# The key mask moved into the score accumulation, and two instead of three expert-sum buffers with smaller prefetch windows

## The chip, the cores and the metric

The kernel runs on one core of one Trainium2 chip. The metric is the device time of one execution in microseconds (us). Engines are named as the profile does: PE is TensorE's matmul, PEld its weight load, DVE is VectorE, ACT is ScalarE, POOL is GpSimd and SP is SyncE, whose instructions are almost all DMA issues ("q" behind an engine's name is its sequencer).

## The reference, cut to what matters

Four layers of gated cross attention and feed-forward run over `x` of shape (16, 128, 256), 2048 tokens, in float32. The two places that the change touches are the first attention (layer 0, 16 heads over 128 keys per sample, with a key mask that is all true in the inputs) and the last feed-forward (layer 3, 64 experts, top 8, capacity-limited):

```python
x = x + jnp.tanh(g_xattn[0]) * _L0_xattn_ref(_layernorm(x, axis=-1), ctx_1024, mask_BxS2_bf1, Wq, Wk, Wv, Wo)
...
# layer 3 feed-forward
xe = jnp.zeros((E, C, H), x.dtype).at[flat_e, pos].set(x_rep, mode='drop')
gu = jnp.einsum('ech,ehf->ecf', xe, gate_up_proj)
g, u = jnp.split(gu, 2, axis=-1)
h = jax.nn.silu(g) * u
ye = jnp.einsum('eci,eih->ech', h, down_proj)
y = jnp.sum(y_flat.reshape(-1, K, H) * topw.reshape(-1, K)[..., None], axis=1)
```

In the layer-0 attention a masked key's score is driven to a huge negative number before the softmax; `any_key` zeroes a sample without a single valid key.

## The kernel before, in words

The work is one long program; each engine has its own instruction stream, written out in order by hand, and the streams meet at counting semaphores (`done(engine, signal, body, item)` waits for one item of a signal). Nothing is planned at run time.

**Layer-0 attention** (`wide_pe`, `wide_act`, `wide_dve`, `wide_pool`, run by `wide_run` for `L0`). Tokens are taken in four blocks `s` of 512 (four samples), and each block has 16 heads, so there are 64 steps of one head on one block. Step `t` is a software pipeline: PE makes the q of head `t` (two float32 matmuls of 512 columns, into bank B4), transposes the probabilities of head `t-4` (line 552), makes the scores of head `t-1` (four matmuls of 128 columns into the four quarters of bank B5, line 565), adds head `t-5` to the output Y (two matmuls of 512 columns), and makes o of head `t-4` (four matmuls of 128). All matmuls are recorded at the helper's line 129, transposes at their own. DVE then adds the mask to the whole bank B5 in place (line 686), takes the maximum over keys (line 687) and scales it (line 693); ACT takes the exponentials (line 635); DVE makes the reciprocal sums; POOL normalizes (line 722). Each DVE result is followed by a wait on its own chain semaphore (`link`). PE may overwrite B5 only once `p_ready` of the head before has come, that is, after ACT has read B5. The mask, as a bf16 additive bias on all 128 partitions, is made once at the start (line 3187) from a copy of the mask bytes broadcast to 128 partitions.

**Zeroing of internal DRAM tables** (`rows_init`): at the start SP queues plain DMAs that blank the row tables and the sum buffers of the three routed feed-forwards. SP then waits for the end of the layer-0 attention before it goes on.

**Layer-3 feed-forward** (`f3_sp`, `f3_pe`, `f3_act`, `f3_dve`, `f3_pool`). Experts 0 to 63 are taken in order. For expert `e`, SP loads its 128 routed rows (row width 324 floats) into slot `e % XR` of `f3_xe` (XR = 12; line 2744); before it does, it waits until the sum of expert `e - XR` has landed. PE transposes the rows (line 2902), makes gate and up, later the down product; ACT copies and takes silu (lines 2926, 2932); DVE multiplies (line 2939) and scales the result into slot `e % YR` of `f3_y` (YR = 4; line 2946), for which it waits until the sum of expert `e - 4` has landed. POOL then issues an indirect DMA that adds the 128 result rows into an internal DRAM buffer `acc[e % AC]` (AC = 3; line 2892). Two additions into one buffer may not be under way together, so POOL waits before expert `e` until the addition of expert `e - AC` has landed. This "scatter-add" is what the text calls a scatter. Expert weights sit in 16 slots (GE = 16), the first 16 experts' are loaded long before, and the rest are loaded by SP in groups of QE = 2 experts between the row loads (lines 2727 and 2729), each group once the last expert that used its slots is through. At the end SP reads the three buffers back in four parts (12 loads, line 2754), DVE adds them (line 2954, two additions a part), adds the gated sum to x (line 2956), and SP stores the output (line 2758).

Of the kernel before, what the change touches and what calls it, by code (L numbers as in the profile page):

```python
# [14 lines left out]
P = 128  # L15
# [36 lines left out]
def _build(nc, ctx, a, out):  # L52
# [56 lines left out]
    ident = sb("ident", [P, P])  # L109
    gates = sb("gates", [P, 8])  # L110
# [44 lines left out]
    mask_bias = tile(R2, 17000, 1024).bitcast(BF16)  # L155

# [125 lines left out]
    class Wide:  # L282


        def __init__(self, name, stage, kv_heads, wq, wk, wv, wo, rms):
# [22 lines left out]
            self.chain = signal("attn_chain", HEADS * (2 if rms else 4))  # L308
# [225 lines left out]
    def wide_pe(pe, S, beside=None):  # L534
# [4 lines left out]
        for t in S.steps:  # L539
# [112 lines left out]
    def wide_dve(dve, S, beside=None):  # L652
        A, s = S.A, S.s

        link = S.chain(dve, A.chain, 1 if A.rms else 6, s)
        if S.ahead or S.old_ahead:
            k_link = Chain(dve, A.k_chain, s + 1, -1 if S.old_ahead else 0)
        for t in S.steps:
# [23 lines left out]
            if S.has(h):  # L682
                i = h % 2
                done(dve, A.s_mm, s, h)
                if not A.rms:
                    link(nc.vector.tensor_tensor(B5, B5, mask_bias[:, tok(S.of(h))], ALU.add))
                link(nc.vector.tensor_reduce(mx[:, i, :], B5.rearrange("p (b k) -> p b k", b=TB), AX.X, ALU.max))  # L687
                if A.rms:
                    done(dve, A.rq_ready, s, h)
                    nc.vector.scalar_tensor_tensor(negm[:, i, :], mx[:, i, :], -1.0, rq[:, i, :], ALU.mult, ALU.mult)\  # L690
                        .then_inc(A.negm_ready.sem, 1)
                else:
                    nc.vector.tensor_scalar(negm[:, i, :], mx[:, i, :], -SCALE_WIDE, None, ALU.mult)\  # L693
                        .then_inc(A.negm_ready.sem, 1)
# [767 lines left out]
    AC = 3  # L1462
    xrows = nc.dram_tensor("f3_rows", (SLOTS, ROW3), F32, kind="Internal").ap()
    acc = [nc.dram_tensor(f"moe_sum{i}", ((B + 1) * P, D), F32, kind="Internal").ap() for i in range(AC)]
    xrows_of = xrows.rearrange("(p e) c -> p e c", e=L3E)
    tables_of_rows = [(F.dram.rearrange("(b p) c -> p b c", p=P), F.acc) for F in (F1, F2)] + [(xrows_of, acc)]
    row_inits = 16 * sum(len(sums) + -(-rows.shape[1] // ROW_BLOCKS) for rows, sums in tables_of_rows)
# [7 lines left out]
    def rows_init(sp, rows, sums):  # L1475
# [3 lines left out]
        for sum_of in sums:  # L1479
            sp.dma_start(sum_of.rearrange("(b p) d -> p b d", p=P), row_blank[:, 0:D].unsqueeze(1).broadcast_to([P, B + 1, D]))\  # L1480
                .then_inc(rows_zeroed, 16)
# [1167 lines left out]
    XR = 12  # L2649
# [3 lines left out]
    QE = 2  # L2653
# [8 lines left out]
    class R3:  # L2662
# [34 lines left out]
    f3_sum = [tile(R1, i * B * D, B * D).rearrange("p (b d) -> p b d", b=B) for i in range(AC)]  # L2697
# [13 lines left out]
    rows_sems = [(x.sem, x.end) for x in kb_in + F2.tile_in[2:]] + [(semaphore(f"f3_rows_in{i}"), 0) for i in range(XR - TG)]  # L2711
    f3_rows_in = [Signal(sem, 16 * -(-L3E // XR), 1, base) for sem, base in rows_sems]
    f3_added = [Signal(sem, 16 * -(-(L3E - i) // AC), 1, base) for i, (sem, base) in
                enumerate([(x.sem, x.end) for x in F2.added] + [(semaphore("f3_added2"), 0)])]
# [23 lines left out]
    def f3_sp(sp):  # L2738
        for sig in rows_written:
            sp.wait_ge(sig.sem, sig.end)  # L2740
        for e in range(L3E):
            if e >= XR:
                done(sp, f3_added[(e - XR) % AC], 0, 16 * ((e - XR) // AC) + 15)
# [5 lines left out]
        for sig in f3_added:  # L2749
            sp.wait_ge(sig.sem, sig.end)  # L2750
# [136 lines left out]
    def f3_pool(pool):  # L2887
        for e in range(L3E):
            done(pool, f3_y_ready, 0, e)
            if e >= AC:  # L2890
                done(pool, f3_added[e % AC], 0, 16 * (e // AC) - 1)
            nc.gpsimd.indirect_dma_start(acc[e % AC], bass.IndirectOffsetOnAxis(ap=f3_xe[:, e % XR, D:D + 1].bitcast(U32), axis=0),
                                         f3_y[:, e % YR, :], None,
                                         bounds_check=(B + 1) * P - 1, compute_op=ALU.add).then_inc(f3_added[e % AC].sem, 16)
# [39 lines left out]
    def f3_dve(dve):  # L2934
        for j in range(L3E + 2):
# [13 lines left out]
    def f3_end_dve(dve):  # L2949
        for j in range(NS):  # L2950
            b = slice(j * TB, (j + 1) * TB)
            dve.wait_ge(sum_in[j], 64 + 16 * AC)
            for i in range(1, AC):
                nc.vector.tensor_tensor(f3_sum[0][:, b], f3_sum[0][:, b], f3_sum[i][:, b], ALU.add).then_inc(sum_chain, 1)
                dve.wait_ge(sum_chain, j * (AC - 1) + i)
# [6 lines left out]
    def _(sp):  # L2962
# [3 lines left out]
        mask = a["mask_BxS2_bf1"].rearrange("b k -> (b k)").rearrange("(o n) -> o n", o=1)  # L2966
        sp.dma_start(mask_all, mask.broadcast_to([P, B * P])).then_inc(in_small, 16)
# [113 lines left out]
    def _(pe):  # L3081
# [9 lines left out]
        pe.wait_ge(const_made, 1)  # L3091
# [41 lines left out]
    def _(act):  # L3133
        act.wait_ge(go, 1)
        act.wait_ge(in_small, 48)
# [41 lines left out]
    def _(dve):  # L3177
# [8 lines left out]
        dve.wait_ge(in_small, 48)  # L3186
        nc.vector.tensor_scalar(mask_bias, mask_all, 1.0, NEG_BIG, ALU.subtract, ALU.mult).then_inc(mask_ready, 1)
# [54 lines left out]
```

## Time and profile before

| what | value |
|---|---|
| median of 3 runs | 2602.42 us (2602.17 to 2604.09) |
| the profiled execution's own time | 2602.42 us |
| its span, first to last instruction | 2600.7 us |
| PE busy | 2179.0 us (84%) |
| DVE busy | 1282.5 us (49%) |
| ACT busy | 1143.6 us (44%) |
| POOL busy | 1058.1 us (41%) |
| mean granted TensorE clock | 0.931 of full speed |

The row loads' line in the page gives KB each and the median us from issue to landing. The span leaves out 1.7 us that lie around the first and last instruction. Busy time on PE is modelled from pipelined records, so neighbouring records overlap: the distance between two starts says what a matmul costs, its duration does not. The layer-0 attention lies between about 66 and 430 us of the span, the layer-3 feed-forward between about 2412 and 2601 us.

### The profile page before, as it was taken

The numbers are of one execution on the slowest core, as the hardware profiler recorded it, in microseconds if no ns is written. First come the engines' busy times: TensorE is split into PE (matmuls) and PEld (weight loads), VectorE is DVE, ScalarE is ACT, GpSimd is POOL, SyncE is SP. The second block draws the span as 40 slices with busy tenths as digits, with TensorE's granted clock in tenths as the row PEclk, the third lists the DMA queues.
The fourth block names the chain that finished last, engine by engine and source line by source line (L and its number), as shares of the span: only waits on it lengthen the run. The fifth ranks groups of instructions, "written<-read, shape, count | busy, mean of one in ns | idle before, by whom it ended". The sixth has DMA issues, their size and how long they took to land.

```text
span 2600.7 us, 37681 instructions
## 1 busy us (share of the span) xinstructions
PE 2179.0 (84%) x11449; PEld 1517.5 (58%) x11449; DVE 1282.5 (49%) x3474; ACT 1143.6 (44%) x3509; POOL 1058.1 (41%) x899
## 2 busy tenths in 40 slices
PE   5999999789999978959999999888995788771773
PEld 4566666657667645636666566446663566551663
DVE  2545554466766663336565554343335365552223
ACT  3444444245545543335665555223332575550221
POOL 1112211033344344534444544324555337656564
PEclk9999999899999998979999999899997899885887
DMA  9999200200000033630000000335667002110898
GB/s 351 358 350 335 81 1 1 66 1 1 1 18 16 3 89 72 100 107 1 1 1 10 27 14 23 120 116 97 102 105 178 9 9 73 62 46 2 200 239 203
DMA packets 218720, 233.18 MB, mean 90 GB/s; under 512 B 31451, under 2 KB 210419, under 8 KB 217756
## 3 DMA queue, kind: packets, MB, share of 16 engines
q1 hardware_dynamic: 181276, 182.62, 23.3%
q0 software_dynamic: 37248, 48.14, 10.1%
q8 instruction: 98, 1.61, 0.3%
q14 instruction: 98, 0.80, 0.1%
HBM read 95.36 MB, written 143.85 MB: 92 GB/s over the span
## 4 chain that ended last, share of the span: by engine, by line
PE 25%; issue 9%; POOL 8%; DVE 6%; DMA 5%; ACT 2%; SPq 1%; POOLq 0%; DVEq 0%; ACTq 0%
PE ps L129 20%; POOL f_rows L2784 4%; DMA moe_sum<-work 4%; POOL weights L2629 2%; PE ps L552 1%; PE ps L578 1%; PE ps L1870 1%; PE ps L1885 1%; POOL rk L437 1%; DMA f_rows<-ctx,weights 1%; ACT work L635 1%; PE ps L406 1%; PE ps L1635 0%; SPq L2754 0%; DVE mx L687 0%
## 5 line engine op out<-in xcount | busy, mean ns | idle before, releaser
L129 PE MATMUL ps<-weights,work 128*128 128x126 f32 (+7 forms) x3328 | 701.4, 344 | 55.5 <-DVE work L2946 29.6
L129 PEld LDWEIGHTS ps<-weights,work 128*128 128x128 f32 (+2 forms) x3328 | 472.4, 195 | 114.5 <-issue 59.9
L129 PE MATMUL ps<-work,weights 128*128 128x512 f32 (+3 forms) x1456 | 494.1, 466 | 3.2 <-ACT work L644 3.2
L129 PE MATMUL ps<-xn_T,weights 128*128 128x512 f32 (+5 forms) x1056 | 381.6, 496 | 12.8 <-DVE weights L1146 6.7
L129 PEld LDWEIGHTS ps<-work,weights 128*128 128x128 f32 (+2 forms) x1456 | 224.6, 189 | 88.1 <-issue 74.8
L1948 POOL DMA_INDIRECT f_sum<-work x120 | 184.9, 1541 | 191.7 <-ACT work L1909 148.9
L722 POOL TENSOR_TENSOR work<-work,rinv 128x512 f32<-128x512 f32 x128 | 133.3, 1042 | 296.6 <-DVE rinv L670 273.6
L129 PEld LDWEIGHTS ps<-xn_T,weights 128*128 128x128 f32 (+3 forms) x1056 | 166.7, 189 | 113.7 <-issue 96.4
L1018 POOL TENSOR_TENSOR work<-weights,head_sel 128x512 f32<-128x512 f32 x128 | 134.3, 1053 | 228.2 <-PE ps L129 200.3
L968 ACT ACTIVATE work<-ps,n_negm 128x128 f32<-128x128 f32 x512 | 145.6, 371 | 133.6 <-DVE n_negm L995 130.2
L635 ACT ACTIVATE work<-ps,negm,rq 128x128 f32<-128x128 f32 x256 | 113.8, 454 | 148.6 <-DVE negm L690 148.6
L129 PE MATMUL ps<-weights 128*128 128x256 f32 (+6 forms) x546 | 148.2, 395 | 22.6 <-DMA weights<-weights 7.3
L635 ACT ACTIVATE work<-ps,negm 128x128 f32<-128x128 f32 x256 | 90.6, 366 | 151.8 <-DVE negm L693 151.8
L2784 POOL DMA_INDIRECT f_rows<-ctx,weights x128 | 128.7, 1006 | 57.2 <-issue 38.2
L129 PEld LDWEIGHTS ps<-work 128*128 128x128 f32 x1024 | 129.6, 192 | 34.5 <-issue 31.6
L993 DVE TENSOR_REDUCE n_mx<-ps 128x4 f32<-128x512 f32 x128 | 88.2, 689 | 116.6 <-PE ps L129 115.0
L2487 ACT ACTIVATE work<-ps,n_negm 128x112 f32<-128x112 f32 (+1 forms) x512 | 112.9, 346 | 72.4 <-DVE n_negm L2556 72.3
L728 POOL TENSOR_TENSOR rq<-qvar,neg_half 128x4 f32<-128x4 f32 x64 | 68.7, 1074 | 185.8 <-DVE qvar L699 185.7
L678 DVE COPY work<-ps 128x512 f32<-128x512 f32 x128 | 88.3, 690 | 100.4 <-PE ps L552 99.8
L129 PE MATMUL ps<-work 128*128 128x128 f32 x1024 | 135.4, 275 | 1.8 <-DVE work L678 1.8
L1560 POOL DMA_INDIRECT f_rows<-xn,weights x96 | 98.6, 1027 | 75.5 <-DVEq L1549 51.4
L2629 POOL TENSOR_TENSOR weights<-weights,neg_half 128x32 f32<-128x32 f32 x16 | 87.1, 5443 | 98.0 <-DVE weights L2581 98.0
(313 smaller groups left out, 3538.5 us busy)
## 6 DMA issues: line engine op xcount, KB each, us to landing
f_rows<-weights SPq DMA_DIRECT2D x25, 2176.0 KB, 19.6
work<-f_rows SPq DMA_DIRECT2D x120, 136.0 KB, 2.5
weights<-in_L_ffn_gate_up_proj SPq DMA_DIRECT2D x32, 384.0 KB, 4.9
f_rows<-weights SPq DMA_DIRECT2D x4, 2592.0 KB, 24.8
work<-f_rows SPq DMA_DIRECT2D x64, 162.0 KB, 4.4
f_sum<-weights SPq DMA_DIRECT2D x4, 2176.0 KB, 16.4
weights<-in_L_ffn_W SPq DMA_DIRECT2D x96, 88.0 KB
moe_sum<-weights SPq DMA_DIRECT2D x3, 2176.0 KB, 17.9
```

Of the source, the lines that this page charges most:

```text
L129: return nc.tensor.matmul(out, lhsT, rhs, start=start, stop=stop, skip_group_check=True)
L635: last = nc.scalar.activation(p_sb[:, h % 4, b * P:(b + 1) * P], B5[:, b * P:(b + 1) * P], ACT.Exp, bias=negm[:, h % 2, b:b + 1], scale=rq ...
L678: nc.vector.tensor_copy(pt_sb, B6).then_inc(A.pt_ready.sem, 1)
L722: nc.gpsimd.tensor_tensor(out=pv, in0=pv, in1=rinv[:, h % 2, :].unsqueeze(2).broadcast_to([P, TB, P]), op=ALU.mult).then_inc(A.pn_ready.se ...
L968: last = nc.scalar.activation(n_p[:, i, j, :], S_BANKS[t % 3][:, j * P:(j + 1) * P], ACT.Exp, bias=n_negm[:, i, j:j + 1], scale=scale)
L993: link(nc.vector.tensor_reduce(n_mx[:, t % 4, 0:NB], S_BANKS[t % 3].rearrange("p (h k) -> p h k", h=NB), AX.X, ALU.max))
L1018: nc.gpsimd.tensor_tensor(out=s_kblk[:, g % KB_RING, :, :], in0=k_t[:, hf, b * P:(b + 1) * P].unsqueeze(1).broadcast_to([P, NB, P]), in1=h ...
L1560: nc.gpsimd.indirect_dma_start(F.dram, bass.IndirectOffsetOnAxis(ap=F.slot_u[:, t, k:k + 1], axis=0), XN[:, t, :], None, bounds_check=F.ro ...
L1948: nc.gpsimd.indirect_dma_start(F.acc[j % 2], bass.IndirectOffsetOnAxis(ap=t_xe[:, j, D:D + 1].bitcast(U32), axis=0), t_y[:, j % 4, :], Non ...
L2487: last = nc.scalar.activation(n_p[:, i, j, lo:hi], S_BANKS[t % 3][:, j * P + lo:j * P + hi], ACT.Exp, bias=n_negm[:, i, m:m + 1], scale=SC ...
L2629: nc.gpsimd.tensor_tensor(out=l3_r[:, b % 2, :], in0=l3_var[:, b % 2, :], in1=neg_half[:, 0:32], op=ALU.pow)\
L2784: nc.gpsimd.indirect_dma_start(xrows, bass.IndirectOffsetOnAxis(ap=f3_slot_u[:, s % 2, t, k:k + 1], axis=0), f3_rows[s % 2][:, t, :], None ...
```

## The change

There are two independent edits.

In the layer-0 attention the addition of the mask on DVE is gone. PE instead opens the accumulation in bank B5 with one bf16 matmul of 512 columns, whose stationary operand is a 128 by 128 tile that holds ones in partition 0 and zeros elsewhere (`ones_b`), and whose moving operand is the mask bias of the block, now filled in partition 0 only and zero elsewhere. The four score matmuls add to it. The start of the program has one DMA more (the mask as a single row), and DVE three small fills more.

In the layer-3 feed-forward there are two sum buffers instead of three, 8 row slots instead of 12, and weights come in groups of 4 experts instead of 2. The row slots and sums have their semaphores accordingly; the end reads and adds two buffers.

```diff
@@ wide_pe
                 done(pe, A.p_ready, s, i - 1)
                 if A.rms:
                     done(pe, A.k_ready, s, i // 4 * 4 + 3)
+                else:
+                    mm(B5, ones_b[:], mask_bias[:, tok(S.of(i))], True, False)
...
-                    last = mm(B5[:, b * P:(b + 1) * P], q_sb[:, i % 2, b * P:(b + 1) * P], keys)
+                    last = mm(B5[:, b * P:(b + 1) * P], q_sb[:, i % 2, b * P:(b + 1) * P], keys, A.rms, True)
@@ wide_dve
                 done(dve, A.s_mm, s, h)
-                if not A.rms:
-                    link(nc.vector.tensor_tensor(B5, B5, mask_bias[:, tok(S.of(h))], ALU.add))
                 link(nc.vector.tensor_reduce(mx[:, i, :], B5.rearrange("p (b k) -> p b k", b=TB), AX.X, ALU.max))
@@ rows_init
-    acc = [... for i in range(AC)]
+    acc = [... for i in range(2)]
@@ layer 3, sizes
-    XR = 12
+    XR = 8
...
-    QE = 2
+    QE = 4
@@ f3_sp
             if e >= XR:
-                done(sp, f3_added[(e - XR) % AC], 0, 16 * ((e - XR) // AC) + 15)
+                done(sp, f3_added[e % 2], 0, 16 * ((e - XR) // 2) + 15)
             sp.dma_start(f3_xe[:, e % XR, :], xrows_of[:, e, :]).then_inc(f3_rows_in[e % XR].sem, 16)
...
-            for i in range(AC):
+            for i in range(2):
                 sp.dma_start(f3_sum[i][:, b], ...).then_inc(sum_in[j], 16)
@@ f3_pool
             done(pool, f3_y_ready, 0, e)
-            if e >= AC:
-                done(pool, f3_added[e % AC], 0, 16 * (e // AC) - 1)
-            nc.gpsimd.indirect_dma_start(acc[e % AC], ...
+            done(pool, f3_added[e % 2], 0, 16 * (e // 2) - 1)
+            nc.gpsimd.indirect_dma_start(acc[e % 2], ...
@@ f3_dve
                 if e >= YR:
-                    done(dve, f3_added[(e - YR) % AC], 0, 16 * ((e - YR) // AC) + 15)
+                    done(dve, f3_added[e % 2], 0, 16 * ((e - YR) // 2) + 15)
@@ f3_end_dve
-            for i in range(1, AC):
-                nc.vector.tensor_tensor(f3_sum[0][:, b], f3_sum[0][:, b], f3_sum[i][:, b], ALU.add).then_inc(sum_chain, 1)
+            nc.vector.tensor_tensor(f3_sum[0][:, b], f3_sum[0][:, b], f3_sum[1][:, b], ALU.add).then_inc(sum_chain, 1)
@@ start, SP
+        sp.dma_start(mask_row[0:1, :], mask).then_inc(in_small, 16)
         sp.dma_start(mask_all, mask.broadcast_to([P, B * P])).then_inc(in_small, 16)
@@ start, DVE
-        dve.wait_ge(in_small, 48)
-        nc.vector.tensor_scalar(mask_bias, mask_all, 1.0, NEG_BIG, ALU.subtract, ALU.mult).then_inc(mask_ready, 1)
+        nc.vector.memset(mask_bias, 0.0)
+        nc.vector.memset(ones_b[:], 0.0).then_inc(const_made, 1)
+        dve.wait_ge(const_made, 2)
+        nc.vector.memset(ones_b[0:1, :], 1.0).then_inc(const_made, 1)
+        dve.wait_ge(in_small, 64)
+        nc.vector.tensor_scalar(mask_bias[0:1, :], mask_row[0:1, :], 1.0, NEG_BIG, ALU.subtract, ALU.mult).then_inc(mask_ready, 1)
```

## Rows read from the trace of the kernel before

**Rows 1.** The page: DMA busy in tenths over 40 slices, and the row loads' issues.

```profile
DMA  9999200200000033630000000335667002110898
...
work<-f_rows SPq DMA_DIRECT2D x64, 162.0 KB, 4.4
```

**Rows 2.** Windows: stretch, busy of PE, PEld, DVE, ACT, POOL, granted clock, DMA share, GB/s.

```profile
160.00:250.00 90.00, 90.00 (x454) 59.42 (x453) 47.66 (x126) 42.98 (x157) 18.22 (x18) 1.00 1.09 345
2440.00:2540.00 100.00, 75.92 (x486) 68.06 (x485) 28.85 (x82) 25.00 (x82) 62.57 (x41) 0.88 1.01 242
```

**Rows 3.** Timeline of one layer-0 step, PE and DVE: start, us, engine, line.

```profile
199.78 1.88 PE L129 MATMUL ps<-xn_T,weights 128*128 128x512 f32 x4
...
201.50 0.60 PE L552 MATMUL ps<-ident,work 128*128 128x128 f32 x4
...
201.94 1.06 PE L129 MATMUL ps<-ctx_T,work 128*128 128x128 f32 x8
...
202.83 1.88 PE L129 MATMUL ps<-work,weights 128*128 128x512 f32 x4
203.03 0.70 DVE L686 TENSOR_TENSOR ps<-ps,weights 128x512 f32<-128x512 f32 x1 [0.20 <-PE ps L129]
...
204.55 1.05 PE L129 MATMUL ps<-work 128*128 128x128 f32 x8
...
205.44 1.88 PE L129 MATMUL ps<-xn_T,weights 128*128 128x512 f32 x4
```

**Rows 4.** Timeline, PE at the scores of heads 1 and 3 of block 0.

```profile
72.62 1.13 PE L129 MATMUL ps<-ctx_T,work 128*128 128x128 f32 x8 [1.64 <-ACT work L635]
...
81.58 1.13 PE L129 MATMUL ps<-ctx_T,work 128*128 128x128 f32 x8 [1.19 <-ACT work L635]
```

**Rows 5.** PE groups by shape, 160 to 250 us, and the widest bf16 group: busy, mean ns.

```profile
L129 PE MATMUL ps<-work,weights 128*128 128x512 f32 x63 | 29.7, 593 | 0.0
...
L129 PE MATMUL ps<-weights 128*128 128x64 bf16 x40 | 2.7, 204 | 4.3 <-DVE weights L2862 2.3 <-DVE x_res L2602 2.0
```

**Rows 6.** Timeline of the start: DVE at the mask, PE at the first weights.

```profile
14.59 1.23 DVE L3187 TENSOR_SCALAR weights<-work 128x2048 bf16<-128x2048 uint8 x1 [3.98 <-DMA gates<-in_g_ffn]
...
27.93 1.97 PE L334 MATMUL ps<-ident,weights 128*128 128x128 f32 x8 [10.67 <-DMA weights<-in_L_xattn_Wq]
```

**Rows 7.** The scatters of the span (line 2892): duration ns, first and last start, landing.

```profile
L2892 POOL DMA_INDIRECT moe_sum<-work x64: 1542/1554/1588, 2422.6 to 2568.0; - x64
...
DMA to landing us min/median/max: 3.7/5.5/8.3
```

**Rows 8.** The same line, stretch 2440 to 2540: issue to landing.

```profile
DMA to landing us min/median/max: 3.8/6.1/8.3
```

**Rows 9.** The same line, stretch 2549 to 2570: first and last start, issue to landing.

```profile
L2892 POOL DMA_INDIRECT moe_sum<-work x12: 1543/1556/1566, 2547.6 to 2568.0; - x12
...
DMA to landing us min/median/max: 3.7/3.8/3.9
```

**Rows 10.** Timeline, 2441 to 2447: row and weight issues, and two scatters.

```profile
2441.24 3.45 SPq L2744 DMA_DIRECT2D work<-f_rows  x2
...
2442.04 1.55 POOL L2892 DMA_INDIRECT moe_sum<-work  x1 [1.42 <-DVE work L2946]
...
2446.77 0.44 SPq L2727 DMA_DIRECT2D weights<-in_L_ffn_gate_up_proj  x1
...
2447.01 1.56 POOL L2892 DMA_INDIRECT moe_sum<-work  x1 [0.30 <-issue]
```

**Rows 11.** The chain that ended last, 2440 to 2470: start, us, what.

```profile
2447.01 7.01 DMA moe_sum<-work
```

**Rows 12.** Timeline of the end: the read-back issues, first and last part on DVE.

```profile
2571.87 14.52 SPq L2754 DMA_DIRECT2D weights<-moe_sum  x12
2579.45 2.48 DVE L2954 TENSOR_TENSOR weights<-weights 128x1024 f32<-128x1024 f32 x2 [14.68 <-DMA weights<-moe_sum]
...
2593.52 2.48 DVE L2954 TENSOR_TENSOR weights<-weights 128x1024 f32<-128x1024 f32 x2 [0.54 <-DMA weights<-moe_sum]
```

More of the change, by code:

```diff
@@ L109, in _build @@
     ident = sb("ident", [P, P])
+    ones_b = sb("ones_b", [P, P], BF16)
     gates = sb("gates", [P, 8])
@@ L307, in __init__ @@
             self.y_mm = signal("attn_y_mm", HEADS)
-            self.chain = signal("attn_chain", HEADS * (2 if rms else 4))
+            self.chain = signal("attn_chain", HEADS * (2 if rms else 3))
             if rms:
@@ L653, in wide_dve @@
         A, s = S.A, S.s
-        link = S.chain(dve, A.chain, 1 if A.rms else 6, s)
+        link = S.chain(dve, A.chain, 1 if A.rms else 5, s)
         if S.ahead or S.old_ahead:
@@ L1461, in _build @@
     SLOTS = P * L3E
-    AC = 3
     xrows = nc.dram_tensor("f3_rows", (SLOTS, ROW3), F32, kind="Internal").ap()
-    acc = [nc.dram_tensor(f"moe_sum{i}", ((B + 1) * P, D), F32, kind="Internal").ap() for i in range(AC)]
+    acc = [nc.dram_tensor(f"moe_sum{i}", ((B + 1) * P, D), F32, kind="Internal").ap() for i in range(2)]
     xrows_of = xrows.rearrange("(p e) c -> p e c", e=L3E)
     tables_of_rows = [(F.dram.rearrange("(b p) c -> p b c", p=P), F.acc) for F in (F1, F2)] + [(xrows_of, acc)]
-    row_inits = 16 * sum(len(sums) + -(-rows.shape[1] // ROW_BLOCKS) for rows, sums in tables_of_rows)
+    row_inits = 16 * sum(2 + -(-rows.shape[1] // ROW_BLOCKS) for rows, _ in tables_of_rows)
     def rows_blank(ordered):
@@ L1478, in rows_init @@
         sp.wait_ge(blank_made, 1)
-        for sum_of in sums:
-            sp.dma_start(sum_of.rearrange("(b p) d -> p b d", p=P), row_blank[:, 0:D].unsqueeze(1).broadcast_to([P, B + 1, D]))\
+        for i in range(2):
+            sp.dma_start(sums[i].rearrange("(b p) d -> p b d", p=P), row_blank[:, 0:D].unsqueeze(1).broadcast_to([P, B + 1, D]))\
                 .then_inc(rows_zeroed, 16)
@@ L2696, in _build @@
     f3_y = tile(WK, 5120, YR * D).rearrange("p (n d) -> p n d", n=YR)
-    f3_sum = [tile(R1, i * B * D, B * D).rearrange("p (b d) -> p b d", b=B) for i in range(AC)]
+    f3_sum = [tile(R1, i * B * D, B * D).rearrange("p (b d) -> p b d", b=B) for i in range(2)]
     in_f3r = semaphore("in_f3r")
@@ L2710, in _build @@
     f3_w_in = [Signal(semaphore(f"f3_w_in{i}"), 32, NG, 0) for i in range(GE // QE)]
[L2711 to L2714, printed above, removed]
+    f3_rows_in = [Signal(semaphore(f"f3_rows_in{i}"), 16 * L3E // XR, 1, 0) for i in range(XR)]
+    f3_added = [Signal(F2.added[i].sem, 16 * L3E // 2, 1, F2.added[i].end) for i in range(2)]
     f3_xt_tr = signal("moe_xt_tr", L3E, 1)
@@ L2748, in f3_sp @@
                 f3_weights(sp, last // GE + 1, last % GE // QE)
-        for sig in f3_added:
-            sp.wait_ge(sig.sem, sig.end)
+        for i in range(2):
+            sp.wait_ge(f3_added[i].sem, f3_added[i].end)
         for j in range(NS):
             b = slice(j * TB, (j + 1) * TB)
-            for i in range(AC):
+            for i in range(2):
                 sp.dma_start(f3_sum[i][:, b], acc[i].rearrange("(b p) d -> p b d", p=P)[:, b]).then_inc(sum_in[j], 16)
@@ L2889, in f3_pool @@
             done(pool, f3_y_ready, 0, e)
[L2890 to L2892 removed]
+            done(pool, f3_added[e % 2], 0, 16 * (e // 2) - 1)
+            nc.gpsimd.indirect_dma_start(acc[e % 2], bass.IndirectOffsetOnAxis(ap=f3_xe[:, e % XR, D:D + 1].bitcast(U32), axis=0),
                                          f3_y[:, e % YR, :], None,
[L2894 removed]
+                                         bounds_check=(B + 1) * P - 1, compute_op=ALU.add).then_inc(f3_added[e % 2].sem, 16)
     def f3_pe(pe):
```

9 lines of the change are left out of this document (5 added, 4 removed).

## The prediction

> **What bounds the kernel now.** I read the page first, for where the DMA engines are full [rows 1]: the first slices, where tables are blanked, and the last four, where layer 3's experts run. The windows come next, one for each of the two places that the change touches [rows 2]. From 160 to 250 us, inside the layer-0 attention, PE is busy 90.00 of 90 us at full clock, DVE 47.66. From 2440 to 2540 us, among the experts, PE has idle time and the DMA share is 1.01, while 41 scatters go by (POOL's count): 2.44 us an expert. After 2549 us the last weights are in, and 12 scatters start from 2547.6 to 2568.0, 1.85 us apart [rows 9].
>
> Then one step of the attention in the timeline [rows 3]. From one q matmul to the next, PE starts are 1.72 (q), 0.44 (transposes), 0.89 (scores), 1.72 (Y) and 0.89 us (o) apart: 5.66 us, without a wait. So PE paces these steps, and DVE's mask addition of 0.70 us lies beside PE's work on Y. Only the first heads differ: there PE idles 1.64 and 1.19 us until ACT's exponentials are through [rows 4], since Y and o are not there yet to fill the time.
>
> Last, the scatters' own lines [rows 7 to 10], the chain [rows 11] and the end [rows 12].
>
> **The mask on PE.** The change adds 64 bf16 matmuls of 512 columns to the engine that paces, and takes 64 additions of 0.70 us from one that does not. No bf16 matmul of that width is in the trace. A float32 matmul of 512 columns is two records (four for the two of q), 1.72/4 = 0.43 us apart [rows 3]. bf16 is one record [rows 5]. Dear bound: one float32 record, 0.43 us. Cheap bound: nothing, if it slips into overlap. I take half a float32 record, 0.215 us, because the 64-column bf16 group already takes 204 ns against 593 for the 512-column float32 record [rows 5], so most of a short matmul is not streaming. Loading the ones should be hidden, as each of the score matmuls' loads is.
>
> The Trainium skill's page "TensorE: Matmul & The Clock Gate", section "Back-to-back issue gap", gives 512 columns about 216 ns isolated and 131 ns in a sustained stream of loads and matmuls; with 131 ns the 58 steps below would cost 7.6 us instead of 12.5. The float32 records 0.43 us apart are two passes' worth of the isolated figure, which is why I don't lean on the smaller one; no bf16 row here decides.
>
> The sum by heads: the first score starts 0.2 us later. The next three intervals are set by DVE and ACT, which lose 0.70 + 0.03 us (the addition and its link) and gain 0.21: -0.52 each, within PE's idle 1.19 to 1.64. The fourth has about half that, -0.25. The 58 paced intervals cost 58 x 0.215 = +12.5. The last has a small idle that takes the mask: -0.1. Together +0.2 - 1.6 - 0.25 + 12.5 - 0.1 = **+10.7 us**, bounds -2 to +23.
>
> **At nothing.** DVE's new fills lie where it waits 3.98 us for the gates, and the mask bias conversion is as long as before along its row. The added mask DMA moves SP's later issues by less than a microsecond; the first weights, for which PE waits 10.67 us, come out of a saturated DMA stretch [rows 1, 6], so a single 2 KB row costs at most its issue. Without this cover it would be 0.5 to 2 us. The missing blanking DMA (2.2 MB) ends before SP's wait for the end of the attention, and nobody waits for it.
>
> **Two sum buffers.** POOL may start scatter e once scatter e-2 has landed. The restart takes 0.8 us: SP's row load, which waits on the landing of scatter 6, goes out at 2441.24, and POOL's scatter 9, which waits on the same landing, starts at 2442.04 [rows 10]. So each buffer turns around in (landing + 0.8), and an expert costs half of it.
>
> After the weights are in, the landing is 3.8 us [rows 9]: (3.8 + 0.8)/2 = 2.3 us an expert. Before, the same stretch went at 1.85 us, near POOL's own 1.56 an issue [rows 9]. Under load the landing is 3.8 to 8.3, median 6.1; over all 64 it is 5.5 [rows 7, 8]. What it will be is the main unknown. Fewer scatters in flight and a slower pace thin out the traffic; but a weight group is now 4 experts (1.2 MB) in one go, and a scatter issued right behind half as much landed after 7.01 us [rows 10, 11]. I take the span's median 5.5: (5.5 + 0.8)/2 = 3.15 us.
>
> How many experts see the load: weight groups go out with row loads 9 to 53, which are released by scatters 1 to 45, so some 43 of the 63 intervals are loaded and 20 are not. 43 x 3.15 + 20 x 2.3 = 181.5 us from first to last scatter, against 2568.0 - 2422.6 = 145.4 before [rows 7]: **+36 us**. Floor for the loaded part: the DMA engines' own 2.44 us, since the bytes per expert stay (43 x 2.44 + 46 = 150.9, +5.5). Ceiling: the landing stays at 6.1 (3.45 us; 194.4, +49).
>
> **Row slots and groups** cost nothing beside this: from the landing that frees a slot, eight experts at 3.15 us are 25 us, and the row load (4.4 [rows 1]), the three PE steps from transpose to result (75.92 us of PE for 41 experts, 1.85 each [rows 2]), DVE's y with the waits around it (1.5) and the landing (5.5) take some 17. If the buffers did not bind, this ring would hold the pace at 17/8 = 2.1 us, below the floor. Behind the waiting row load in SP's queue stand the weight groups; they are used 11 experts later, over 30 us. POOL's wait holds nothing else in POOL's queue. DVE's wait for e-4 stays; it ends earlier than POOL's own.
>
> **The end.** The four parts reach DVE 14.07/3 = 4.69 us apart with three loads each [rows 12], 1.56 us a load. One load less per part is -6.3, one addition of 1.24 less after the last is -1.2: **-7.5 us**, bounds -5 (the additions alone) and -9.
>
> **Sum.** +10.7 + 36 - 7.5 = +39. The profiled execution took 2602.42 us (span 2600.7 and 1.7 around it), the same as the median of the runs. 2602.4 + 39.2 = **2641.6 us**.
>
> **Rivals.** (a) *The DMA engines are the only bound.* A share of 1.01 [rows 2] speaks for it: if a scatter doesn't wait behind bulk loads, two buffers could turn in 4.6 us, and the loaded part stays at its floor of 2.44. Then +10.7 + 5.5 - 7.5: 2611. Against it speaks the landing of 7.01 us behind a weight group [rows 11]. The skill's page "DMA: Bandwidth & Descriptors", section "Queues, rings and completion order", says that each engine round-robins between its queues at packet granularity, so a scatter would wait for about a packet, however large the group; by that rule this rival's time would hold. The 7.01 us is more than the 3.8 of the quiet stretch by 3.2, so the trace doesn't bear the rule out well here.
>
> (b) *The landing stays long.* Groups of twice the size hit the scatter released by the same landing each time; at 6.1 us median, +10.7 + 49 - 7.5: 2654.5.
>
> (c) *The clock drops.* It was 0.88 of full in the loaded stretch, with PE 76% busy [rows 2]. With more idle time it may fall to 1.2 GHz for longer, and 1.85 us of PE an expert at 0.88 is 1.63 at full and 3.26 at half. For the 20 light intervals wholly at half clock that is 20 x (3.26 - 2.3) = +19: 2661.
>
> (d) *Not slower.* If the attention's 5.66 us were not PE's own but a loop through DVE's addition, with the idle time hidden in modelled ends, its removal would take 0.52 us off each of 62 intervals: -32 instead of +10.7, in all 2602.4 - 32 + 36 - 7.5 = 2599. It decides from a saving of 0.46 us a step. Against it: the five starts of [rows 3] add up to matmul costs, and the early heads, where that loop does rule, have visible idle time [rows 4].
>
> **Chances and range.** The forecast (landing between 5 and 6 us) 0.45; (a) 0.2; (b) 0.17; (c) 0.11; (d) 0.03; something small that I mis-sized the other way, 0.04. The range reaches down to just above (a), whose middle cases belong in it, and up past (b) and (c) by the dear mask: 2610 to 2666. A change under 0.2% (5 us) can't be told from none in this kernel. Faster 0.03, same 0.04, slower 0.93.
>
> **What would show it.** In the changed profile: the attention's step at 5.66 + 0.21 us with PE still full; DVE's addition gone and no shorter stage; the first heads' intervals near 4.0 instead of 4.48; POOL waiting on the sums' DMA in most experts, which before it did rarely; scatter starts in the loaded stretch 3.15 apart and 2.3 in the light one, with landings of 5.5 and 3.8; a DMA share there of 2.44/3.15, about 0.77; the end's parts 3.1 us apart. A share still at 1.0 would mean (a) or costlier packets; granted clock below 0.8, (c). The prediction is wrong at its root if POOL's waits don't grow, or if the attention gets shorter.

## The result, and the profile after

The changed kernel takes 2669.66 us (median of 4 runs, 2661.15 to 2670.46) against 2602.42: ratio 1.025, 95% interval 1.0228 to 1.0271. The direction was forecast; the size was not (+67 us against +39), and the time lies just above the range of 2610 to 2666. The profiled execution took 2665.1 us with a span of 2663.4, 62.7 us more than before, and that is what the comparison below divides up.

In the attention the step is as forecast. The timeline of PE shows the new bf16 record 0.21 us ahead of the scores, and from one q to the next it is 5.88 us (206.73 to 212.61), against 5.66 [rows 3] (start, us, engine, line, as there):

```profile
206.73 1.88 PE L130 MATMUL ps<-xn_T,weights 128*128 128x512 f32 x4
208.45 0.60 PE L554 MATMUL ps<-ident,work 128*128 128x128 f32 x4
208.89 0.38 PE L130 MATMUL ps<-weights,ones_b 128*128 128x512 bf16 x1
209.10 1.05 PE L130 MATMUL ps<-ctx_T,work 128*128 128x128 f32 x8
210.00 1.88 PE L130 MATMUL ps<-work,weights 128*128 128x512 f32 x4
211.72 1.05 PE L130 MATMUL ps<-work 128*128 128x128 f32 x8
212.61 1.88 PE L130 MATMUL ps<-xn_T,weights 128*128 128x512 f32 x4
```

The windows (columns as in [rows 2]) show the attention as full as before and DVE with less to do, but the loaded expert stretch at 31 scatters in 100 us instead of 41, with the DMA engines at 0.79 and the granted clock at 0.76:

```profile
160.00:250.00 90.00, 89.63 (x445) 59.87 (x451) 35.39 (x105) 43.50 (x154) 17.34 (x18) 1.00 1.10 345
2440.00:2540.00 100.00, 63.45 (x348) 56.31 (x348) 19.78 (x58) 18.42 (x58) 47.46 (x31) 0.76 0.79 174
```

The scatters' line, over the whole span, answers to [rows 7]: 204.9 us from the first start to the last, against 145.4, and 73.5 us of POOL's idle time ended by a sum's landing. The landings are known for one buffer's 32 scatters only:

```profile
L2890 POOL DMA_INDIRECT moe_sum<-work x64: 1542/1554/1592, 2434.4 to 2639.3; - x64
its engine sat idle before it (us, times) until:
  DMA moe_sum<-work: 73.5, 21
...
DMA to landing us min/median/max: 3.7/4.1/9.2
```

The waits between 2434 and 2640 us name a second candidate: PE waited for row loads 25 times, 72.6 us in all, which it did not do before (who waited, for what: us, times, longest):

```profile
PE ps L2900 <- DMA work<-f_rows: 72.6, 25, 5.1
POOL moe_sum L2890 <- DMA moe_sum<-work: 73.5, 21, 7.4
```

The timeline around one weight group shows both at once. The group goes out from 2536.35 (its down weights at 2536.89). Scatter 31 starts at 2536.78 and scatter 32 at 2538.84, both into the group's traffic. The next scatter needs scatter 31's buffer, and POOL waits 7.07 us for it. It starts at 2547.44, 0.8 us after the row load at 2546.64 that waits on the same landing:

```profile
2536.35 0.50 SPq L2726 DMA_DIRECT2D weights<-in_L_ffn_gate_up_proj  x1
2536.78 1.55 POOL L2890 DMA_INDIRECT moe_sum<-work  x1 [1.12 <-DMA moe_sum<-work]
...
2538.84 1.54 POOL L2890 DMA_INDIRECT moe_sum<-work  x1 [0.50 <-issue]
...
2547.44 1.55 POOL L2890 DMA_INDIRECT moe_sum<-work  x1 [7.07 <-DMA moe_sum<-work]
2549.30 1.54 POOL L2890 DMA_INDIRECT moe_sum<-work  x1 [0.30 <-issue]
```

The end answers to [rows 12]. From the first read-back issue to the end it is 20.4 us (2643.0 to the span's 2663.4) against 28.8, the parts 3.0 us apart instead of 4.69:

```profile
2643.00 7.23 SPq L2753 DMA_DIRECT2D weights<-moe_sum  x8
2648.50 1.23 DVE L2951 TENSOR_TENSOR weights<-weights 128x1024 f32<-128x1024 f32 x1 [14.19 <-DMA weights<-moe_sum]
...
2657.49 1.23 DVE L2951 TENSOR_TENSOR weights<-weights 128x1024 f32<-128x1024 f32 x1 [0.44 <-DMA weights<-moe_sum]
```

So the 62.7 us are: 11.8 until the first scatter starts (8.3 of it at the attention's last head, by the start of its maximum, 427.66 to 436.00), +59.5 from the first to the last scatter, and -8.4 at the end; the remaining -0.2 is the last landing. The 3.5 us between the attention and layer 3 are not accounted for. Eight profiles with the attention as before, from chips where the kernel before takes 2602 to 2606 us, have their first scatter between 2422.6 and 2432.2 us, so a difference of 3.5 says nothing.

### The profile page after: what moved, and what is told of

Its sections match the earlier page's. It is cut to its first block, busy times and chain, and to the rows that moved or that the text cites. A ratio compares the mean times of both kernels' runs of the same rounds, so it can differ in the third digit from the quotient of the medians.

```text
span 2663.4 us, 37680 instructions
## 1 busy us (share of the span) xinstructions
PE 2210.3 (83%) x11482; PEld 1545.2 (58%) x11513; DVE 1232.2 (46%) x3409; ACT 1150.0 (43%) x3509; POOL 1057.8 (40%) x899
## 4 chain that ended last, share of the span: by engine, by line
PE 25%; issue 9%; DMA 8%; POOL 7%; DVE 6%; ACT 2%; SPq 1%; POOLq 0%; DVEq 0%; ACTq 0%
PE ps L130 20%; DMA moe_sum<-work 5%; POOL f_rows L2783 4%; POOL weights L2630 2%; DMA work<-f_rows 1%; PE ps L554 1%; PE ps L582 1%; PE ps L1871 1%; PE ps L1886 1%; POOL rk L439 1%; DMA f_rows<-ctx,weights 1%; ACT work L639 1%; PE ps L408 1%; PE ps L1636 0%; DVE mx L689 0%
## 5 line engine op out<-in xcount | busy, mean ns | idle before, releaser
L130 PE MATMUL ps<-work,weights 128*128 128x512 f32 (+3 forms) x1456 | 504.6, 475 | 2.7 <-ACT work L648 2.7
L130 PEld LDWEIGHTS ps<-work,weights 128*128 128x128 f32 (+2 forms) x1456 | 234.8, 196 | 89.9 <-issue 75.3
L2890 POOL DMA_INDIRECT moe_sum<-work x64 | 99.2, 1550 | 118.6 <-DMA moe_sum<-work 73.5
```

Source lines behind the costliest of these rows:

```text
L130: return nc.tensor.matmul(out, lhsT, rhs, start=start, stop=stop, skip_group_check=True)
L2890: nc.gpsimd.indirect_dma_start(acc[e % 2], bass.IndirectOffsetOnAxis(ap=f3_xe[:, e % XR, D:D + 1].bitcast(U32), axis=0), f3_y[:, e % YR, : ...
```

## The experiments

The runs came on several chips, and the kernel before takes 2602 to 2606 us on some and 2645 to 2650 on others. So a total is given as a ratio to the kernel before on the same chip, and theories about layer 3 are judged by the stretch from the first to the last scatter's start, which lay between 144.8 and 147.1 us in each of the four experiments here that left its code alone. "Stretch" means this below.

Theory 1 is the forecast's: the turnaround of two buffers sets the pace, slots and groups cost nothing of their own. Theory 2 came from the waits above: row loads stand behind the large weight group, 8 slots let them be issued too late, and PE, which takes experts in order, stands still. Theory 3 came up after eight runs: a scatter issued behind a weight group waits for the whole group, and only with two buffers is every such wait paid. Each stretch below comes from one profiled execution. The changed kernel and layer 3 alone have the same sizes and give 204.9 and 209.5 us, so differences under 5 us are not read.

**The attention alone** (the edit of `wide_pe`, `wide_dve` and the start, in the kernel before).

> The kernel before with the attention's edit alone (mask as a bf16 matmul on PE, DVE's addition gone), layer 3 as before. The two theories below are about layer 3 and agree here: the step goes from 5.66 to 5.87 us, in all +8 to +11 us, 2611 to 2613 us. If the mask's matmul also disturbed later stages, more than +13.

Measured: 2651.61 against 2647.24 us, ratio 1.0019 (1.0007 to 1.0031): +4.4, below the +8 to +11. Steps of 5.87 us, as forecast. The stretch is untouched (2472.0 to 2616.8).

**Layer 3 alone.**

```diff
-    AC = 3
+    AC = 2
-    XR = 12
+    XR = 8
-    QE = 2
+    QE = 4
```

> The kernel before with all three sizes of layer 3 changed (2 buffers, 8 row slots, groups of 4) and the attention as before. Scatters took 59.5 us more in the changed kernel and the end 8.4 us less: +48 to +54 us, 2650 to 2656 us, by both theories. Together with the attention's edit alone it should add up to the whole change (+60 to +67).

Measured: ratio 1.0166 (1.014 to 1.0192), +48 us on medians (2695.61 against 2647.24). The stretch is 209.5 us (2469.5 to 2679.0). It carries most of the change; with the attention's +4 the sum is +53 here, short of the +60 to +67 expected and of the +67 that the whole change measured on the first chip.

**One size at a time, and two at a time.** Each kernel changes only the sizes named.

```diff
-    AC = 3
+    AC = 2
```

> Only the sum buffers go from 3 to 2; 12 row slots and groups of 2 stay. Theory 1 (the turnaround of two buffers, landing + 0.8 us, sets the pace whatever the slots and groups): nearly all of layer 3's cost is here, 2640 to 2652 us. Theory 2 (most of the loss beyond the turnaround is a row load that stands behind a 1.2 MB weight group and is late because only 8 slots let it be issued so late; PE, which takes experts in order, stands still): here only the turnaround and the light end cost, about 43 x 0.3 + 20 x 0.45 - 8.4 = +13 us, 2610 to 2622 us, and PE hardly waits for row loads.

Ratio 1.0097 (1.0074 to 1.0119), +25 us on medians: between theory 2's +8 to +20 and theory 1's +38 to +50, so neither had the total. The stretch is 178.6 us: +33, close to the forecast's +36 for the buffers. PE waits for rows only once, at the start, as theory 2 had said.

```diff
-    XR = 12
+    XR = 8
```

> Only the row slots go from 12 to 8; 3 buffers and groups of 2 stay. Theory 1 and the step of my prediction that put the slots at nothing: within 3 us of 2602. Theory 2: PE waits for row loads behind 0.6 MB groups, some microseconds each second expert: +5 to +20 us, 2607 to 2622 us.

Ratio 1.0039 (1.0023 to 1.0055), stretch 158.2 us. With three buffers the slots do cost 13 us, and PE waits for rows (31 times, 37.1 us). Theory 1's 3 us are out, theory 2's +5 to +20 us hold.

```diff
-    QE = 2
+    QE = 4
```

> Only the weight groups go from 2 to 4 experts; 3 buffers and 12 slots stay. Theory 2 (row loads late behind large groups, but only where 8 slots let them be issued late): 12 slots hide an 8 us row load, so scatters from first to last take 145 to 152 us and PE hardly waits for rows. Rival: the large group in itself delays every scatter landing behind it and costs 10 us or more.

Ratio 1.0046 (1.0028 to 1.0063), stretch 154.9 us: +9.5, between what the two readings had forecast. Its known landings (42):

```profile
DMA to landing us min/median/max: 3.8/6.4/8.3
```

```diff
-    XR = 12
+    XR = 8
-    QE = 2
+    QE = 4
```

> 8 row slots and groups of 4, with 3 buffers. Theory 2: the two multiply: more than the 13 us of the slots alone, 25 to 40 us in the scatter stretch (170 to 185 us), with PE waiting for row loads up to 5 us at a time. Theory of separate costs: the slots' 13 us plus whatever the groups alone cost.

Ratio 1.0092 (1.0067 to 1.0118), stretch 176.5 us (2429.7 to 2606.2): more than the two costs of 13 and 9.5 together, and inside theory 2's 170 to 185. So far theory 2 looked right.

```diff
-    AC = 3
+    AC = 2
-    QE = 2
+    QE = 4
```

> 2 buffers and groups of 4, with 12 slots. Theory 2: little more than the 2 buffers alone, 178.6 us from first to last scatter: 179 to 188, POOL waiting on the sums' landing, PE not on rows. If landings behind a 1.2 MB group are what made the changed kernel slower than forecast (my record's unknown landing), this stretch is 195 us or more.

This one fells theory 2. With 12 slots PE waits for rows only once, at the start, and yet the stretch is 209.2 us, as long as with 8; ratio 1.0199 (1.0177 to 1.0221). The chain that ended last shows where it goes (start, us, what): scatters that take turns at some 8 and 3.8 us. (It passes from one buffer's scatters to the other's.)

```profile
2523.30 8.13 DMA moe_sum<-work
...
2533.49 3.73 DMA moe_sum<-work
...
2538.04 7.52 DMA moe_sum<-work
...
2545.70 3.83 DMA moe_sum<-work
...
2550.35 9.60 DMA moe_sum<-work
...
2560.76 3.77 DMA moe_sum<-work
```

The scatters' line of the same kernel has the longest landing of all:

```profile
DMA to landing us min/median/max: 3.7/3.9/10.6
```

This trace has all 64 landings, and with them it can be seen what each scatter waited for. Of the 62 that follow another in their buffer, 32 start 0.8 us after that one's landing, 26 right behind POOL's scatter before, and 4 come 1.1 to 1.6 us after the landing. DVE's result (line 2946) was ready at least 2.3 us earlier each time, so neither PE, nor the row slots, nor the four slots of `f3_y` held one up. With three buffers and 8 slots it is the other way: DVE's result ends less than 1 us before its scatter in 37 of 61, with groups of 4 in 27 of 61.

```diff
-    AC = 3
+    AC = 2
-    XR = 12
+    XR = 8
```

> 2 buffers and 8 slots, with groups of 2. Both waits are on one loop: a row load waits for the landing of e-8, PE for the row, POOL for the landing of e-2. Theory 2: somewhat above the larger of the two, 180 to 192 us from first to last scatter; if costs simply added, 178.6 + 13 = 192.

Ratio 1.0086 (1.0061 to 1.0111). The stretch is 174.5 us, not longer than with 12 slots, though PE waits for rows 47 times. It lies just below what theory 2 had given (180 to 192). The scatters' line, with groups of 2 (32 landings):

```profile
L2892 POOL DMA_INDIRECT moe_sum<-work x64: 1542/1554/1587, 2424.2 to 2598.7; - x64
...
DMA to landing us min/median/max: 3.7/4.8/6.0
```

**Smaller groups with two buffers.** Single experts' loads, their pair's wait as before:

```diff
-        es = bass.ds(g * GE + q * QE, QE)
+        es = bass.ds(g * GE + q, 1)
...
-            if last >= 0 and last % QE == QE - 1 and last // QE + GE // QE < L3E // QE:
+            if last >= 0 and last + GE < L3E:
                 done(sp, f3_y_mm, 0, last)
-                f3_weights(sp, last // GE + 1, last % GE // QE)
+                f3_weights(sp, last // GE + 1, last % GE)
```

> 2 buffers, 12 slots, and the weights expert by expert (0.3 MB at a time, same bytes). Theory 3, formed from the runs so far: a scatter issued behind a weight group waits for the whole group, and with 2 buffers each such wait is paid. Groups of 4 gave landings of 8 to 9 us behind a group and 209 us from first to last scatter, groups of 2 some 5 us and 178.6; so groups of 1 give landings of about 4.5 us and 165 to 173 us. Rival (engines switch between queues after a packet, so a group's size is indifferent and the 30 us between groups of 4 and 2 have another cause): 177 to 181 us.

A miss for theory 3's number, and above the rival's too: stretch 183.9 us (2471.5 to 2655.4), ratio 1.0097 (1.0069 to 1.0124). From 2 down to 1 nothing is gained with two buffers; the jump is between 2 and 4. The timeline (scatter 30, then the row load of expert 42, which waits for scatter 30's landing) shows why:

```profile
2562.87 1.54 POOL L2892 DMA_INDIRECT moe_sum<-work  x1 [2.76 <-DVE work L2946]
...
2567.94 0.34 SPq L2744 DMA_DIRECT2D work<-f_rows  x1
2568.32 0.43 SPq L2727 DMA_DIRECT2D weights<-in_L_ffn_gate_up_proj  x1
2568.74 1.54 POOL L2892 DMA_INDIRECT moe_sum<-work  x1 [2.47 <-DVE work L2946]
...
2569.74 0.43 SPq L2727 DMA_DIRECT2D weights<-in_L_ffn_gate_up_proj  x1
...
2570.59 1.56 POOL L2892 DMA_INDIRECT moe_sum<-work  x1 [0.31 <-issue]
```

The weights of two experts go out 1.4 us apart, released by a pair of landings, and then none for some 4.5 us. So each pair of scatters meets the same 0.6 MB as with groups of 2, and scatter 30 lands after 5.1 us, not 4.5.

**The weight groups on another queue.**

```diff
-                done(sp, f3_y_mm, 0, last)
-                f3_weights(sp, last // GE + 1, last % GE // QE)
...
+                last = e - 4
+                if last >= 0 and last % QE == QE - 1 and last // QE + GE // QE < L3E // QE:
+                    done(act, f3_y_mm, 0, last)
+                    f3_weights(act, last // GE + 1, last % GE // QE)
```

> All three sizes of layer 3 as in the changed kernel (2 buffers, 8 slots, groups of 4), attention as before, but the weight groups are issued from ACT's queue, at about the same time, so that row loads no longer stand behind them in SP's queue. Theory 2 (late row loads behind the group cost the time): PE's waits for rows vanish and the stretch falls from 205 to 209 us to 175 to 190. Theory 3 (scatters land late behind the group and 2 buffers pay for it): scatters stay behind the same bytes, 200 to 212 us, even if PE's waits for rows shrink.

Stretch 199.0 us (2462.2 to 2661.2), ratio 1.0154 (1.0127 to 1.0182). PE's waits for rows stay (62.9 us), so they did not come from the order within SP's queue, and the stretch shrinks by only 6 to 10 us, to just below theory 3's 200 to 212. It speaks against theory 2 again.

**No weight loads at all, in both versions.** The output is not the reference's: experts 16 to 63 use the weights of the first 16.

```diff
-            if last >= 0 and last % QE == QE - 1 and last // QE + GE // QE < L3E // QE:
-                done(sp, f3_y_mm, 0, last)
-                f3_weights(sp, last // GE + 1, last % GE // QE)
...
-                if e % QE == 0:
+                if e % QE == 0 and e < GE:
                     done(pe, f3_w_in[e % GE // QE], e // GE, 31)
```

> All three sizes of layer 3 changed (2 buffers, 8 slots, groups of 4), but the weights of experts 16 to 63 are not loaded: the first 16 experts' weights are used again, so the output is not the reference's. Nothing but row loads and scatters is left on the DMA engines. Theory 3 (the cost of 2 buffers beyond their quiet turnaround is landings behind weight groups): landings of 3.8 to 4.2 us, 2.3 to 2.45 us an expert, 146 to 155 us from first to last scatter instead of 205 to 209. Rival (8 slots and PE's order hold it up even so): 165 us or more, with PE waiting for rows.

> The kernel before with the same weight loads left out (output not the reference's). 3 buffers then run at POOL's pace of 1.86 us: 117 to 122 us from first to last scatter instead of 145.4. The difference to the run before this one is the quiet price of two buffers, 64 x 0.45 = 28 us; of the 60 us that layer 3's edit costs, the other half belongs to the weight groups.

The scatters' line with 2 buffers, 8 slots, groups of 4 and no loads:

```profile
L2889 POOL DMA_INDIRECT moe_sum<-work x64: 1542/1554/1592, 2425.2 to 2581.7; - x64
...
DMA to landing us min/median/max: 3.7/3.8/5.5
```

and of the kernel before without loads (21 landings):

```profile
L2889 POOL DMA_INDIRECT moe_sum<-work x64: 1542/1555/1593, 2432.2 to 2554.2; - x64
...
DMA to landing us min/median/max: 3.8/4.6/5.4
```

156.5 against 122.0 us: just above theory 3's 146 to 155 and below the rival's 165, and at the upper end of 117 to 122. Without weights, the three sizes cost 34.5 us; the weights add 23.4 to the kernel before (145.4) and 48.4 to 53.0 to the changed one (204.9 and 209.5). Totals: ratios 1.0018 (1.0004 to 1.0032) and 0.9908 (0.9881 to 0.9936). The quiet price of two buffers is above the 28 us that I had expected.

**Two thirds of the group's bytes.** Two buffers, 12 slots, groups of 4, later groups without the down weights (output not the reference's, the first 16 experts' down weights serve all).

```diff
+        if g == 0:
             sp.dma_start(f3_dn[:, q * QE:(q + 1) * QE], ...)
```

> 2 buffers, 12 slots and groups of 4, but of the later groups only gate and up are loaded (0.8 MB instead of 1.2; the down weights of experts 0 to 15 are used again, output not the reference's). Landings behind a 1.2 MB group were 8 to 9 us, behind 0.6 MB about 5. If the whole group stands before the scatter, its landing is 6 to 7 us here and the stretch 180 to 192 us. If it is not the bytes but four experts in one issue that matter, the stretch stays at 200 to 209.

```profile
L2893 POOL DMA_INDIRECT moe_sum<-work x64: 1542/1554/1592, 2429.1 to 2613.2; - x64
...
DMA to landing us min/median/max: 3.7/4.4/7.8
```

184.1 us: still four experts in one issue, but 0.8 MB instead of 1.2, and the stretch falls by 25 us, with the longest landing at 7.8 us instead of 10.6. With two buffers it is the bytes in front of the scatter. (This group is also one DMA instead of two, but the groups of 2 are two DMAs as well, and behind them the known landings end within 6.0 us.) Ratio 1.0117 (1.0088 to 1.0145).

**The attention, twice more.** First no mask at all (the mask is all true in the inputs; a false key would not be masked):

```diff
-                if not A.rms:
-                    link(nc.vector.tensor_tensor(B5, B5, mask_bias[:, tok(S.of(h))], ALU.add))
```

> The kernel before without adding the mask in the layer-0 attention at all, neither on DVE nor on PE (the mask is all true in the inputs; a mask with a false key would not be applied). If PE paces the attention, DVE's 64 additions were nearly free: only the first heads gain, 2 to 3 us, ratio 0.9985 to 1.0. If DVE's addition were on the pacing loop: -30 us.

Ratio 0.9987 (0.9969 to 1.0004). The intervals between the first five heads' maxima fall from 4.48 to 3.75, 3.75, 3.84 and 4.21 us, 2.4 us in all, and the later ones stay at 5.66, or 6.10 in 16 of them: DVE's addition was nearly free. Then the attention's edit again:

> The attention's edit alone once more, with more rounds, since the first measurement (+4.4 us, ratio 1.0007 to 1.0031) lay below the +10.7 us of the forecast while its profile showed steps of 5.87 us as forecast. By the steps the attention ends 8 us later: ratio 1.003. If part of it is regained later, because stages behind wait for something else, 1.0015 to 1.002.

Ratio 1.0017 (1.0002 to 1.0032), 2652.24 against 2645.54 us. This lies in the range for "regained later", but the interval holds the other reading's 1.003 too. Both measurements put the edit at some 4 to 7 us by medians, below the 10.7 of the forecast, with intervals that are as wide as the effect.

**Towards a faster kernel.** The early read-back of two buffers:

```diff
-        for sig in f3_added:
-            sp.wait_ge(sig.sem, sig.end)
-        for j in range(NS):
-            for i in range(AC):
+        for i in ((L3E - 3) % AC, (L3E - 2) % AC, (L3E - 1) % AC):
+            sp.wait_ge(f3_added[i].sem, f3_added[i].end)
+            for j in range(NS):
```

> The kernel before, in which the read-back of two of the three sum buffers starts as soon as each has its last addition, and DVE adds these two while the third comes. The read-back's 6.3 MB pace the end (4.69 us a part); now 2/3 of them start 2 to 4 us earlier and only one addition of 1.24 us a part is left after the last load: the end from the last scatter's landing goes from 28.8 to 19 to 23 us, -6 to -10 us in all, ratio 0.996 to 0.998. If the end is bound by bytes alone: -3 us.

No gain: ratio 0.9995 (0.9981 to 1.0009). DVE gets its first part only 12.2 us after the first read-back issue (7.6 before), presumably because four parts of one buffer now come ahead of it (not tested):

```profile
2618.37 15.45 SPq L2753 DMA_DIRECT2D weights<-moe_sum  x12
2630.59 1.23 DVE L2953 TENSOR_TENSOR weights<-weights 128x1024 f32<-128x1024 f32 x1 [15.36 <-DMA weights<-moe_sum]
```

With the expert-by-expert loads of the groups-of-1 diff on top:

> The same with the weights expert by expert. With 3 buffers and groups of 2 the loaded stretch runs at 2.44 us an expert with the DMA engines full, so theory 3 expects little from smaller groups: 141 to 145 us from first to last scatter against 145.4, thus at most 4 us below the run before this one. If landings behind groups still cost with 3 buffers (groups of 4 cost 9.5 us), the stretch falls to 136 to 140.

Ratio 0.9963 (0.9948 to 0.9977), stretch 134.9 us (2474.2 to 2609.1): a gain far above what I had expected of smaller groups with three buffers, and against theory 3's "only with two buffers". So the groups-of-1 diff was run alone, on the kernel before:

> The kernel before with the weights expert by expert as the only edit (3 buffers, 12 slots, old end). With the early read-back this gave ratio 0.9963 and a scatter stretch of 134.9 us against 147.1 without it. So this alone: stretch 134 to 137 us, -8 to -11 us, ratio 0.996 to 0.997. If the gain needed the early read-back as well, 0.998 or more.

Ratio 0.9949 (0.9931 to 0.9967), 2634.27 against 2645.54 us on the same chip, stretch 132.9 us, somewhat better than expected. This kernel, the one before with weights loaded expert by expert, beats both. Its window in the loaded stretch, beside [rows 2]:

```profile
2480.00:2560.00 80.00, 62.75 (x433) 54.47 (x434) 26.59 (x74) 21.74 (x72) 55.85 (x37) 0.98 1.07 268
```

37 scatters in 80 us are 2.16 us an expert, with the DMA share at 1.07 and 268 GB/s instead of 242.

The stretches side by side, us from the first to the last scatter's start:

| buffers, slots | groups of 1 | groups of 2 | groups of 4 | no loads |
|---|---|---|---|---|
| 3, 12 | 132.9 | 145.4 | 154.9 | 122.0 |
| 3, 8 | | 158.2 | 176.5 | |
| 2, 12 | 183.9 | 178.6 | 209.2 | |
| 2, 8 | | 174.5 | 204.9, 209.5 | 156.5 |

## Why the prediction was right or wrong

**The step that failed is the landing in "Two sum buffers".** I took 5.5 us for every loaded scatter, the median of the trace of before. The mechanism was right, (landing + 0.8)/2 an expert: with groups of 2 landings were near 5 us and the pace of the loaded part 2.9 us, and two buffers alone cost 33 us where the forecast said 36. But the change also made the groups 1.2 MB, and behind such a group the landings in the chain above are 7.5 to 9.6 us, for both scatters in flight, while the next pair lands in 3.8. One such pair of turns takes about (8.4 + 0.8) + (3.8 + 0.8) = 13.8 us for four experts, 3.45 an expert, which is rival (b)'s number. In the changed kernel the 12 groups go out from 2440.49 to 2594.35, 14.0 us apart. I had the row that warned of this, 7.01 us behind half the bytes, and averaged it away.

The count was off as well. The last group goes out just before scatters 47 and 48, and the first of these holds up scatter 49. So the first 49 intervals took 171.0 us (2434.4 to 2605.4), 3.49 each, where I had 43 at 3.15 and six at 2.3; that is 21.7 of the 23.4 us by which the stretch exceeded the forecast.

That the bytes of the group are the cause with two buffers is shown by the 0.8 MB run (184.1 against 209.2) and by the pair without loads. It does not carry over to three buffers as it stands: there the longest landing is 8.3 us with groups of 0.6 MB [rows 7] and again 8.3 with 1.2 MB, only the median moves, 5.5 to 6.4, and the stretch grows by 9.5 us.

**The light part** was forecast at 2.3 us an expert. The last 14 intervals of the changed kernel took 33.9 us, 2.42 each, and the changed sizes without any loads 156.5/63 = 2.48. The slots have no part in the latter: DVE's result was ready over 1 us before its scatter in all but one case. The landings do it, 3.8 us in the median but up to 5.5, 4.0 on average: (4.0 + 0.8)/2 = 2.4.

**"Row slots and groups cost nothing"** holds for the slots, beside two buffers only (178.6 and 174.5; 209.2 and 204.9), and is false with three (145.4 and 158.2; 154.9 and 176.5). It is false for going to groups of 4 in either case. I had put the slots' ring at 2.1 us an expert; where three buffers leave it free it runs at 158.2/63 = 2.5, which two buffers' turnaround hides. In the changed kernel DVE's result came less than 1 us before its scatter in only 10 of 62 cases, for all of PE's 72.6 us of waiting.

**The floor of 2.44 us** was wrong as a floor: a DMA share of 1.01 did not mean that no more could pass, as 2.16 us with expert-by-expert loads shows. Part of the 2.44 was a turnaround too: in the trace of before, 20 of 61 scatters start 0.8 us after the landing of the scatter three before, and (6.1 + 0.8)/3 is already 2.3. The floor carried rival (a), which did not come about.

**The attention.** The step was right to the hundredth: the mask's matmul takes 0.21 us of it, so the alternative of 7.6 us in all is out. So was the claim that PE paces and that DVE's work was free but for the first heads. From the first head's maximum to the last one's the attention takes 10.05 us longer in each of the three profiles with the edit, where the forecast had 10.55. The last head came only 8.3 us later because the first maximum started 1.7 us earlier (68.33 against 70.04), where I had 0.5; PE's q before it starts 1.2 us earlier already (65.13 against 66.33), ahead of anything that the edit touches in the attention. In totals the edit measured +4.4 and +6.7 us by medians, with intervals that end at +8.2 and +8.5. Whether a part is regained between the attention and layer 3 is not shown: on the chips of these two measurements and their like the first scatter starts at 2472.0 and 2474.5 us with the edit, and anywhere from 2461.7 to 2474.2 in eight profiles with the attention as before.

**The end** was right: -8.4 against -7.5.

**Rivals.** (a) out. (b) is what happened by mechanism and pace; its total of 2654.5 was still 15 us short. (c): the granted clock did fall to 0.76, the sign that I had named for it, but in the kernel with two buffers, 12 slots and groups of 4 it was 0.76 as well (2440 to 2540 us), and there every result was ready 2.3 us or more before its scatter. So PE's pace did not set the stretch. (d) out by the no-mask run. The Trainium skill's page "DMA: Bandwidth & Descriptors", section "Queues, rings and completion order", describes round-robin between queues at packet granularity; by that rule, as the prediction read it, a scatter's landing would not depend on how large the group in the other queue is. The runs with two buffers differ: longest landing 6.0 us with groups of 0.6 MB, 7.8 with 0.8 and 10.6 with 1.2. What in the chip makes a scatter wait for so many bytes, no run shows.

**What stays open.** The parts measured by themselves (+48 and +4 us) fall short of the whole (+67). They ran on different chips, and the whole was not run on the second one. On a chip nearer to the first, where the kernel before takes 2606 us, two buffers with groups of 4 alone measured +54.6, so the chip may be part of it.

## What to carry to other kernels

When a ring gets fewer buffers, its latency is paid at each turn, so ask what else in the same change makes that latency longer: here a bulk load twice as large in front of it cost as much again as the missing buffer. An average latency hides this; take the row right behind the burst. And a wait that appears in the new profile (PE on rows, 72.6 us) is not yet the cause: giving it back its slots changed nothing. The check that needs no run is to compare, scatter by scatter, when its data was ready with when its buffer came free.

## What the runs showed of the hardware that was not expected

The same bytes in smaller DMAs moved faster though the DMA engines already showed as full: from 242 GB/s at a share of 1.01 to 268 GB/s at 1.07, 145.4 to 132.9 us. The same kernel took 2602 to 2606 us on some chips and 2645 to 2650 us on others, while its layer-3 scatter stretch differed by at most 2.3 us. Splitting a load into smaller DMAs did not spread it in time where the loads were released in pairs, and then the landings stayed as long (5.1 us against about 5).
